# A Mamba scan inside a transformer sandwich: four states by 32 channels in a tile, four 32-column sums together, and a scan that does not stop between sequences

## The reference, cut to what matters

```
x = x + ln(attn(ln(x)))          # bf16, 2 heads, softmax over 512 keys, then relu(y Wo + bo)
x = x + ln(moe(ln(x)))           # bf16, 8 experts, top 2 by sqrt(softplus(score)) + bias, one shared expert
x = x + ln(mamba(ln(x)))         # f32
x = x + ln(ternary_ffn(ln(x)))   # f32, relu squared, rms norm, weights in {-s, 0, s}

mamba:  z, x, B, C, dt = split(h W_in)
        delta = softplus(dt W_dt + 2 b_dt)
        u     = silu(conv4(repeat(x)) + conv_b)             # 512 channels
        state[c, n, t] = exp(delta[c,t] A[c,n]) state[c, n, t-1] + delta[c,t] u[c,t] B[g(c), n, t]
        y[c, t] = sum over n of state[c, n, t] C[c // 16, n, t]      # 16 states n
        out   = ((y + u D) * silu(z)) W_out
```

## Time and profile before

| | |
|---|---|
| median of 3 runs | 2097.48 us (2095.4 to 2104.95) |
| the profiled execution, its own time | 2099.33 us |
| its span, first to last instruction | 2097.5 us |
| busy | PE 1651.5 us (79%), DVE 1770.0 (84%), ACT 1035.9 (49%), POOL 913.8 (44%) |
| PE's granted clock, mean | 0.899 of 2.4 GHz |
| DMA | 157.95 MB, 75 GB/s over the span |

### The profile page before, as it was taken

How to read it: one execution, slowest core, us unless ns; L and a number is a source line. 1 busy time by engine, 2 the same in 40 slices (tenths; PEclk the granted TensorE clock), 3 DMA queues, 4 the chain that set the end, 5 groups by cost and what they waited for, 6 DMA issues and landing times. The chain is left out here.

```text
span 2097.5 us, 22567 instructions
## 1 busy us (share of the span) xinstructions
PE 1651.5 (79%) x5875; PEld 725.3 (35%) x5948; DVE 1770.0 (84%) x3142; ACT 1035.9 (49%) x1745; POOL 913.8 (44%) x676
## 2 busy tenths in 40 slices
PE   3375577778996889868997799878997899779856
PEld 1122123232452335322452335332452335234324
DVE  6577899989879998979989998999989987987830
ACT  3247444825555454735556355734547344734312
POOL 0101534454437434554346434464346544665510
PEclk9977699979997999979997899979997899999978
DMA  4100222222222222222231222222222223223300
GB/s 108 46 0 21 72 79 89 92 69 77 75 92 65 85 71 86 85 67 78 74 101 65 81 76 76 96 75 72 76 96 71 76 85 106 86 99 113 110 10 11
DMA packets 94601, 157.95 MB, mean 75 GB/s; under 512 B 10940, under 2 KB 23660, under 8 KB 94468
## 3 DMA queue, kind: packets, MB, share of 16 engines
q1 hardware_dynamic: 94468, 156.43, 22.9%
HBM read 143.83 MB, written 12.58 MB: 75 GB/s over the span
## 5 line engine op out<-in xcount | busy, mean ns | idle before, releaser
L1226 POOL TENSOR_TENSOR prod<-state,c_all 128x512 f32<-128x512 f32 x512 | 669.6, 1312 | 706.8 <-DVE state L1203 644.0
L1203 DVE TENSOR_TENSOR_SCAN state<-decay,ps_b 128x512 f32<-128x512 f32 x512 | 619.7, 1210 | 9.7 <-issue 0.4
L750 PE MATMUL ps_y<-prod,idf 128*128 128x512 f32 x1024 | 610.6, 689 | 4.8 <-DVE u L1216 3.6
L1210 DVE TENSOR_TENSOR ps_b<-du,ps_b 128x512 f32<-128x512 f32 x512 | 347.7, 679 | 87.3 <-PE ps_b L743 86.8
L919 ACT ACTIVATE decay<-delta,a_neg 128x512 f32<-128x512 f32 x512 | 359.3, 719 | 32.3 <-DVE state L1203 29.3
L743 PE MATMUL ps_b<-b_rows,sel_b 48*128 48x512 bf16 x512 | 209.9, 411 | 155.0 <-DVE state L1203 152.7
L750 PEld LDWEIGHTS ps_y<-prod,idf 128*128 128x128 f32 x1024 | 183.8, 207 | 136.3 <-issue 109.9
L743 PEld LDWEIGHTS ps_b<-b_rows,sel_b 48*128 48x128 bf16 x512 | 47.8, 94 | 467.3 <-DVE state L1203 332.5
L619 PE MATMUL ps_x<-xT,w 128*128 128x512 bf16 (+1 forms) x391 | 132.0, 422 | 80.1 <-DVE arena_l L1095 65.6
L826 ACT ACTIVATE arena_l<-ps_x 128x512 f32<-128x512 f32 (+1 forms) x104 | 61.8, 594 | 190.8 <-PE ps_x L619 189.7
L535 PE MATMUL ps_x<-hT,win 128*128 128x512 bf16 (+1 forms) x455 | 135.6, 441 | 21.4 <-DVE arena_b L1171 16.6
(11 more groups left out here) (230 smaller groups left out, 2422.2 us busy)
## 6 DMA issues: line engine op xcount, KB each, us to landing
c_all<-c_rows SPq DMA_DIRECT2D x512, 256.0 KB
c_rows<-arena_l SPq DMA_DIRECT2D x32, 256.0 KB
out<-arena_b SPq DMA_DIRECT2D x8, 512.0 KB
x_in<-in_base SPq DMA_DIRECT2D x8, 256.0 KB
c_all<-in_winT SPq DMA_DIRECT2D x1, 1280.0 KB, 7.5
arena_b<-in_w_fc SPq DMA_DIRECT2D x1, 1024.0 KB, 5.7
arena_b<-in_w_proj SPq DMA_DIRECT2D x1, 1024.0 KB, 5.0
w<-in_w1T SPq DMA_DIRECT2D x1, 792.0 KB, 5.9
```

The source lines that it names most:

```text
L750: nc.tensor.matmul(ps_y[:], idf[:], prod[:, n % NP, :], start=(n % NST == 0), stop=(n % NST == NST - 1)).then_inc(reduced, 1)
L1203: nc.vector.tensor_tensor_scan(state[:, n % NS, :], decay[:, n % NDA, :], ps_b[:, n % NDB, :], 0.0, ALU.mult, ALU.add).then_inc(scanned, 1)
L1210: nc.vector.tensor_tensor(ps_b[:, j % NDB, :], du[:, slot(s, ct), :], ps_b[:, j % NDB, :], ALU.mult).then_inc(driven, 1)
L1226: nc.gpsimd.tensor_tensor(prod[:, n % NP, :], state[:, n % NS, :], c_all[:, n % NC, :], ALU.mult).then_inc(multiplied, 1)
```

## The change

**Tile.** A tile now holds 4 states of 32 channels. Within a channel tile, tile n takes channels 32q to 32q+31 (q = n mod 4) and states 4p to 4p+3 (p). PE's spreading matmul takes a table `sel_s` of its own, the decay's scale comes from a rearranged `a_neg`, and delta and du must be repeated four times over the partitions: LATE stores both to DRAM (`d_store`, `d_rows`, 2 DMAs of 256 KB a channel tile) and the scan reads them back with four DMAs of 64x512 f32 (128 KB) for each q, in the last four steps before a channel tile begins (`scan_sync`).

**Sum.** For each four tiles PE does four matmuls with 32 output columns each, into partitions 0, 32, 64 and 96 of `ps_y`, at once, where it did one of 128 columns after each tile. They come after the fourth product.

**Slots.** An iteration has 64 steps of full weight and no others; scan steps past the end of a sequence are tiles of the next (`tile_at`). LATE is laid over the first 61 steps, BACK and GATE over those from 6 on. In a slot the chains' steps now come before the scan's instruction.

**Moves.** `shift`, `probs`, both relus, `round` and `eps16` go from DVE to ACT; `d_round` becomes two steps of ACT (`d_one`, `d_less`); `d_fix`, `d_sum` and `gated_y` go to POOL; `d_log` waits for `d_fix`. Eight small temporaries of the router go to PSUM, with one copy more (`gate_twin`).

```
-            if part == 2:
-                for n in sums_at(j):
-                    if n % NST == 0:
-                        wait(eng, y_taken, s.count(PER, n))
-                    eng.wait_ge(multiplied, s.count(PER, n + 1))
-                    nc.tensor.matmul(ps_y[:], idf[:], prod[:, n % NP, :], start=(n % NST == 0),
-                                     stop=(n % NST == NST - 1)).then_inc(reduced, 1)
+            s, n = tile_at(at, j - 3)
+            if part == 2 and exists(s) and n % QN == QN - 1:
+                ct, part_n, q = parts(n)
+                if part_n == 0:
+                    wait(eng, y_taken, s.count(PER, NST * ct))
+                eng.wait_ge(multiplied, s.count(PER, n + 1))
+                for q in range(QN):
+                    ins = nc.tensor.matmul(ps_y[q * QC:(q + 1) * QC, :], sel_y[:], prod[:, (n - QN + 1 + q) % NP, :],
+                                           start=(part_n == 0), stop=(part_n == QN - 1))
+                ins.then_inc(reduced, QN)
...
-        steps += [(k, "P", ("d", i)), (k + 1, "A", ("d_abs", i)), (k + 2, "A", ("d_exp", i)), (k + 3, "A", ("d_log", i)),
-                  (k + 5, "V", ("d_sum", i)), (k + 3, "V", ("d_round", i)), (k + 4, "V", ("d_fix", i)),
-                  (k + 6, "G", ("delta", i)), (k + 7, "G", ("du", i))]
+        steps += [(k, "P", ("d", i)), (k + 1, "A", ("d_abs", i)), (k + 2, "A", ("d_exp", i)), (k + 3, "A", ("d_one", i)),
+                  (k + 4, "A", ("d_less", i)), (k + 5, "G", ("d_fix", i)), (k + 6, "A", ("d_log", i)), (k + 7, "G", ("d_sum", i)),
+                  (k + 8, "G", ("delta", i)), (k + 9, "G", ("du", i)), (k + 11, "S", ("d_store", i))]
...
-                  (b + 6, "V", ("shift", i)), (b + 7, "A", ("exp", i)), (b + 8, "V", ("sum", i)),
-                  (b + 9, "V", ("recip", i)), (b + 10, "V", ("probs", i)),
+                  (b + 6, "A", ("shift", i)), (b + 7, "A", ("exp", i)), (b + 8, "V", ("sum", i)),
+                  (b + 9, "V", ("recip", i)), (b + 10, "A", ("probs", i)),
...
+                for kind, rep in enumerate((delta, du)):
+                    rows = d_rows[s.par, ct, kind].rearrange("(q g o c) t -> q g o c t", q=QN, g=QG, o=1)[q]
+                    for g in range(QG):
+                        eng.dma_start(rep[64 * g:64 * (g + 1), q, :],
+                                      rows[g].broadcast_to([QN, NST, T])).then_inc(d_spread[q], 16)
...
-        SLOTS = [(j, part, 1.0 if 0 <= j <= PER else 0.25) for j in STEPS for part in range(3)]
+        SLOTS = [(j, part) for j in range(PER) for part in range(3)]
+        ALL = [1.0] * len(SLOTS)
+        AHEAD = [1.0 if j < PER - 3 else 0.05 for j, _ in SLOTS]
+        BEHIND = [1.0 if j > Y_LAG else 0.0 for j, _ in SLOTS]
...
-            for k, (j, part, _) in enumerate(SLOTS):
-                fns["scan"](eng, s, j, part)
+            for k, (j, part) in enumerate(SLOTS):
                 for slots in chains:
                     run_steps(e, eng, fns, slots[k])
+                fns["scan"](eng, s, j, part)
```

More of the change, by code:

```diff
@@ L29 @@
 NST = 16
+QN = 4
+QC = P // QN
+QG = QC // NST
 NXB = 4
@@ L822, in late_act @@
                     wait(eng, late["V"], s.count(LPER, 0))
+                    wait(eng, late["G"], s.count(LPER, 0))
+                    for k in range(CT):
+                        wait(eng, d_stored[k], s.count(PER, 0))
                 if i >= 2:
@@ L1459, in program @@
                 iteration(e, eng, fns, Seq(n))
+            for j in range(PER, PER + Y_LAG):
+                for part in range(3):
+                    fns["scan"](eng, Seq(NBATCH - 1), j, part)
             alone(e, eng, fns, tagged("back", Seq(NBATCH - 1), BACK))
```

358 lines of the change are left out of this document (211 added, 147 removed), and 2 rows, old and new, of the table b.

## The result

The changed kernel takes **2594.83 us** (median of 4 runs, 2587.49 to 2600.41), the kernel before 2096.44 in the same set: a ratio of 1.236 (95% interval 1.232 to 1.241). It is slower by 24%, where I had forecast 5% faster. The profiled execution has a span of 2598.6 us; PE's granted clock fell from 0.899 to 0.719, and DMA carries 241.95 MB at 93 GB/s where it was 157.95 MB at 75.

A forecast was written before the change was run, and what follows sets the result against it. DVE, 91% busy in a full iteration with PE at 85%, was taken to set the pace. From 2099.33 us, terms -179.5, +79, -20, +24, -24, +4 and +10 summed to -106.5, giving 1993 us, range 1915 to 2120.

The forecast's parts named there:

- DMAs, +4: SP's queue, 8 stores and 64 reads more a sequence: issues just fit, iteration 7 falls behind; +4 us, bounds 0 and 12.
- Ring of products, +24: POOL's product waits for sums of the previous four tiles, without slack; twice in POOL's stretch: +24 us, bounds 0 and 52.
- DVE work leaving, -179.5: Softplus, attention and gated_y steps leave DVE inside the scan: -179.5 us while DVE is the bound.
- POOL's stretch, +79: Products of tiles 50 to 58: POOL has 34.6 us of work, DVE 21, so DVE stalls; +79 us.
- rival 2: POOL does not bind: its f32 steps fall towards 1.27 us and DVE's lead covers the rest; 1890 us, chance 0.12.
- Rival 3, the hand-overs: Longer chains through ACT and POOL cost 10 us a full iteration, 5 in two others: 2053 us, chance 0.16.
- Between sequences, -24: The scan no longer empties, so seven of eight 3.5 us DVE waits for a sequence's last sum go: -24 us.
- PE's sums, 1.13 us for four: Four 32-column matmuls run side by side in 1.13 us; PE loses 37 us an iteration, DVE's spread waits -20 us.
- rival 1: The four sums run one after another, 3.44 us a group, and PE keeps its load: 2121 us, chance 0.20.
- a drain of the size that the prediction weighed: PE loses 0.27 us of overlap into and out of each group, 69 us in all; -20 becomes nought, 2013 us.
- Rival 4, the clock: PE, less busy, gets 1.2 GHz for longer; its -20 us off DVE's spread waits becomes nought: 2013 us, within the 0.52 forecast.
- Startup, +10: 16 reads go ahead of C's first, delaying the first product by 9.9 us: +10 us, bounds 5 and 20.

The follow-up runs named there:

- the half worth 62 us of DVE time: Kernel before with only shift, probs, relus and roundings on ACT and the router's temporaries in PSUM: 2053.1 us (0.980).
- moves_only: Kernel before with only the moved steps of the change; tile and order between sequences as before: 2158.6 us (1.030).
- with pairs: Changed kernel, reads on sixteen engines, 32-column sums two at a time: 2147.8 us; with moved steps back on DVE (wrong softmax sign) 2090.2 us.
- the early group: Changed kernel, reads on sixteen engines, four sums ahead of the spread of tile 4k+7: 2146.8 us; with moved steps back on DVE 2152.7 us.
- one_row_reads: Changed kernel with each delta and du read after the first channel tile bringing 1 partition instead of 64: 2264.8 us (1.081).
- one_row_single: Changed kernel with one-partition delta and du reads and its 32-column sums one by one: 2190.7 us (1.045).

## Why the prediction was wrong

The predicted 1993 us missed by 602. By its own steps:

- **DMAs, +4: the step that failed most.** I counted SP's issues (five in a step, 3.1 us, "just fits") and a landing of 2.7 us, taken from a weight load. What counts is how long the engines carry the bytes. The reads of a channel tile are 16 DMAs of 128 KB at 98 GB/s, 16 x 1.34 = 21 us, and four loads of C go over the same engines in between, 1.34 us each: 27 us for what four steps of 3.4 us, 13.6 us, have to hide. This estimate gives 6.7 us a tile, and in the timeline above the decays start 6.5 to 6.8 apart. On 16 engines the same reads and C's loads cost 313 us less. The prediction had named this sign of being wrong itself ("the delta reads arriving after DVE asks for them"), and gave it no price above 12 us. A landing of 2.7 us for one DMA alone says nothing about a burst. The place to look was there before the change, C's loads in a short window, here 742 to 760 of the kernel before: they never use more than half of the engines, nor more than 205 GB/s.

```profile
DMA  3452022452000023443000005442113442000424
GB/s 105 168 205 77 0 23 86 173 191 105 5 0 0 0 23 96 164 155 118 27 0 0 0 0 105 173 168 87 50 27 118 164 155 91 27 0 0 36 114 168
```

- **Ring of products, +24: too small, by the group's place in PE's order.** "Where DVE sets the pace POOL has time for it" leaves out that the sum stands behind a spread, and the spread behind a scan two tiles on. That made it 135 us at the old place, once the reads were mended. The upper bound of 52 (56 by its own terms, 2 x 4.0 x 7) was no bound, since it priced the sum and not what PE does before it.
- **DVE work leaving, -179.5: the work left, the time did not.** DVE's busy time is 1560.8 us, as forecast. But I priced it as if DVE alone set the pace, with PE 85% busy beside it and the steps handed through ACT and POOL. In the old tile the moves cost 63 us where this term and the next had them bring 100: the half worth 62 us of DVE time brought 42, the other half cost 105.
- **POOL's stretch, +79: not seen where it was put.** In `moves_only` the stretch from the product of tile 50 to that of tile 58 does grow, from 33.7 us to 40.9, but POOL is not full in it, and neither is DVE:

```profile
1140.16:1181.07 40.91, 24.54 (x78) 7.80 (x77) 24.73 (x38) 31.20 (x45) 30.95 (x23) 0.78 0.20 65
```

  POOL has 31 us of work there, not 34.6, mostly since its softplus steps took 1.27 us and not 1.473 (the condition of rival 2), and it is idle for 10. In the changed kernel it has 32.0 in 39.5. What was seen of the mechanism stands later, in the last 20 us of a sequence (no pause, then the wait of 9.4 us for the last sum), and `gated_y`, alone on POOL, costs 25 us. **Rival 3, the hand-overs**, was the real rival of this term. I put it at 60 us; the softplus through ACT and POOL alone costs 80.
- **Between sequences, -24: wrong.** The gap did shrink to 1.6 us, but the whole kernel became 14 us slower; by the reading above the chains' steps that had filled the gap went into the scan.
- **PE's sums, 1.13 us for four: right.** Eight records of a group span 1.06 us at the full clock and 1.93 at the lower; one sum of before took 1.02 to 1.13 at the full clock. A group at the full clock:

```profile
693.04 1.06 PE L783 MATMUL ps_y<-prod,sel_y 128*32 128x512 f32 x8
```

  They run side by side, and rival 1 has nothing for it. Nor does a drain of the size that the prediction weighed show (0.27 us into and out of each group). A group starts 0.07 us before the record of the spread ahead of it ends (692.72 + 0.39 against 693.04), as a sum did before (1000.46 + 0.39 against 1000.78). The matmul behind this group starts at 694.04, 0.06 before its end; behind a sum of before a projection started 0.16 before (median), so leaving costs 0.1 us a group at most. The Trainium skill's 2.38 times for three ("TensorE: Matmul & The Clock Gate", Part 3) is less than what this trace has, four in the time of one.
- **Rival 4, the clock**, happened, and more strongly than "-20 becomes nought": 0.899 to 0.719, and the spread went from 411 to 489 ns. Packing the sums takes most of it (0.870 with single ones, 0.749 with packed, both with the one-partition reads), and with the late reads it is lower again (0.719 against 0.749). What it costs in time no run isolates.
- **Startup, +10:** it is +28.5. With the reads on sixteen engines it is 21.6; the moves alone give 17.9.

From the changed kernel down, then: 2594.8 - 313 (engines) - 135 (place of the sums) = 2147, then 58 for the moves (with pairs, not with the early group), and 2090 is the best of the new tile here, in a kernel whose softmax has the wrong sign: 8 us under the kernel before in the same set, no more. Its gain on PE goes unused while DVE is 90% busy (212.3 of 236.1 us in iteration 3), and part of it goes into the clock. Against the terms of the sum the misses are 309 for the reads, 111 for the ring, 163 for the moves with POOL's stretch and 38 between sequences. They add up to 621 where the miss is 602, since the runs that price them differ in the rest of the kernel.

## What to carry to other kernels

A DMA that copies rows to several partitions has a shape, and in these traces its first dimension went with how many of the 16 engines worked: look at GB/s and busy share in a window that holds only this kind of transfer, and multiply by the whole burst, before counting issues. When one engine is 91% busy and the next 85%, work taken from the first need not come back as time: here 81 us of DVE's time in five iterations brought 40. And each step put on an idle engine in the middle of a chain adds a hand-over that both busy engines may stand behind; try the moves in halves, since here one half paid and the other lost more. A ring without slack costs what its releaser stands behind, not what the releasing instruction takes.

## What the runs showed of the hardware that I had not expected

- Delta and du reads with 4 as first dimension ran at 98 GB/s and a quarter of the 16 engines, C's loads with 8 at about 190 and a half, and reads with 32 together with C's loads (16) at 271 and 86%. One engine moved 98 / 4 = 24.5 GB/s; with nearly all busy it was 271 / (0.856 x 16) = 19.8 on average over that window, in single slices of which all 16 reached 427 GB/s. A second queue (ACT's) used the same engines and changed nothing in the burst.
- Four f32 matmuls of 32 columns into four partition quarters of a PSUM bank started within 0.02 us of each other and took 1.06 us in all, where one took 1.02 to 1.13.
- The same kernel with its sums packed was granted 0.749 of PE's clock, with single sums 0.870 (`one_row_reads`, `one_row_single`), and its other matmuls were slower for it (fcT 666 ns against 630).
